# Corner products of a deformable convolution moved from VectorE to GpSimd, in place between its gathers, on one Trainium2 core

## The reference, cut to what matters

```python
# one sample: four corners, each with a weight
return gather(y0, x0) * (wy0 * wx0) + gather(y0, x0 + 1) * (wy0 * wx1) \
     + gather(y0 + 1, x0) * (wy1 * wx0) + gather(y0 + 1, x0 + 1) * (wy1 * wx1)
...
samp = _bilinear(h, y, x) * mask[:, None]
out = jnp.einsum('bckhw,ock->bohw', samp, w2.reshape(w2.shape[0], w2.shape[1], 9))
```

## Time and profile before

| what | value |
|---|---|
| median of the timed runs | 629.05 us (3 runs, 628.83 to 629.80) |
| span of the profiled execution, first to last instruction | 852.6 us |
| the profiled execution's own time around its span | not shown |
| busy: PE, DVE, ACT, POOL | 531.5, 353.6, 277.5, 283.4 us |
| POOL's gathers (L309), 288 | 282.2 us busy |
| DVE's products (L1167), 32 | 43.5 us busy |
| DVE's sums (L1180), 32 | 68.9 us busy |

### The profile page before, as it was taken

How to read it: one execution, slowest core, us unless ns; L and a number is a source line. 1 busy time by engine, 2 the same in 40 slices (tenths; PEclk the granted TensorE clock), 3 DMA queues, 4 the chain that set the end, 5 groups by cost and what they waited for, 6 DMA issues and landing times.

```text
span 852.6 us, 7735 instructions
## 1 busy us (share of the span) xinstructions
PE 531.5 (62%) x2840; PEld 362.9 (43%) x2840; DVE 353.6 (41%) x462; ACT 277.5 (33%) x402; POOL 283.4 (33%) x296
## 2 busy tenths in 40 slices
PE   5789930117883065026604897271859998999797
PEld 2445410113542033014502665151636785678576
DVE  4244420002671193129400586151347984752243
ACT  1436510005550041104100554130235633554353
POOL 0000477750037477734775006565520000000000
PEclk8697975558996578556756899585889999999899
DMA  4000111110001121100211001111100000000000
GB/s 166 0 1 1 52 52 53 52 40 26 1 22 53 37 63 52 52 26 22 76 52 43 1 2 40 43 41 43 59 22 0 0 25 0 1 1 16 10 1 25
DMA packets 15298, 27.11 MB, mean 32 GB/s; under 512 B 4900, under 2 KB 9256, under 8 KB 15144
## 3 DMA queue, kind: packets, MB, share of 16 engines
q0 software_dynamic: 9216, 18.89, 7.8%
q1 hardware_dynamic: 5768, 6.20, 2.2%
q10 hardware_dynamic: 288, 1.67, 0.5%
HBM read 22.41 MB, written 4.33 MB: 31 GB/s over the span
## 4 chain that ended last, share of the span: by engine, by line
PE 41%; another core or an unknown queue 30%; DVE 11%; issue 8%; ACT 7%; DVEq 2%; DMA 1%; ACTq 0%
PE ys L559 6%; PE yy L581 5%; PE xq L346 5%; DVE samples L1180 3%; PE yy L572 3%; DVE neg_max L1086 2%; ACT expT L805 2%; PE ys L479 2%; PE xq L319 2%; PE yy L319 2%; PE ys L319 2%; PE xs L325 2%; DVE weighed L1167 2%; PE xq L389 1%
## 5 line engine op out<-in xcount | busy, mean ns | idle before, releaser
L309 POOL DMA_INDIRECT got<-cell_table,rows_cur x288 | 282.2, 980 | 247.5 <-DVE weighed L1167 149.3
L346 PE MATMUL xq<-vT,expT 128*128 128x129 f32 x512 | 68.8, 294 | 14.9 <-ACT oT L898 7.3
L581 PE MATMUL yy<-v3T,probsT 128*128 128x128 f32 x512 | 65.1, 282 | 16.2 <-issue 15.3
L346 PEld LDWEIGHTS xq<-vT,expT 128*128 128x128 f32 x512 | 66.8, 210 | 19.5 <-issue 9.5
L581 PEld LDWEIGHTS yy<-v3T,probsT 128*128 128x128 f32 x512 | 61.7, 196 | 24.5 <-issue 20.2
L1180 DVE TENSOR_REDUCE samples<-weighed 128x288 f32<-128x1152 f32 x32 | 68.9, 2153 | 2.2 <-issue 0.7
L559 PE MATMUL ys<-k,q_offs 128*128 128x512 f32 x112 | 55.1, 616 | 1.3 <-ACT k L924 1.3
L1264 DVE TENSOR_REDUCE neg_max<-ys 128x1 f32<-128x1024 f32 x28 | 34.2, 1222 | 38.6 <-PE ys L559 35.7
L1210 DVE RECIPROCAL inv<-xq 128x1 f32<-128x1 f32 x32 | 5.3, 167 | 103.2 <-remote 68.6
L479 PE MATMUL ys<-samplesT,wts 96*128 96x512 f32 x48 | 29.8, 772 | 27.7 <-issue 27.1
L470 PE MATMUL yy<-wts,samples 128*96 128x128 f32 x72 | 14.1, 313 | 52.2 <-ACT samplesT L800 43.5
(11 more groups left out here) (186 smaller groups left out, 875.4 us busy)
## 6 DMA issues: line engine op xcount, KB each, us to landing
got<-cell_table,rows_cur POOLq DMA_INDIRECT x288
cell_table<-tabS SPq DMA_DIRECT2D x4, 512.0 KB
xall<-x_dram SPq DMA_DIRECT2D x3, 512.0 KB, 9.3
out_dram<-cells SPq DMA_DIRECT2D x3, 512.0 KB, 2.7
wts<-weights_dram ACTq DMA_DIRECT2D x1, 1120.5 KB, 8.9
xall<-x_dram ACTq DMA_DIRECT2D x1, 512.0 KB, 5.0
out_dram<-cells SPq DMA_DIRECT2D x2, 256.0 KB, 2.0
wts<-weights_dram SPq DMA_DIRECT2D x1, 289.0 KB, 4.8
```

The source lines that it names most:

```text
L309: nc.gpsimd.indirect_dma_start(got[:, t, k, :], None, table, bass.IndirectOffsetOnAxis(ap=rows_cur[:, n, at:at + 1], axis=0)).then_inc(got ...
L346: last = nc.tensor.matmul(to, expT[:, j, t * P:(t + 1) * P], vT[:, j, C - width:C + 1], start=j == 0, stop=j == TILES - 1)
L581: last = nc.tensor.matmul(yo[:, 0:C], probsT[:, j * P:(j + 1) * P], v3T[:, j, :], start=j == 0, stop=j == TILES - 1)
```

## The change

A POOL instruction multiplies the gathered corners in place, in the slot of `got`; DVE's product and its buffer go; DVE's sum waits for that product (`weighed`, now a semaphore), reads `got`, and releases slot and table after its drain. On POOL the product of tile t-1 stands behind the nine gathers of tile t; the last tile's product follows its own gathers. A wait for the corner weights stands once an element, ahead of the first product. In the second loop DVE's separate calls of `l1_weigh` go, and `l1_add` stays where it was; wherever `l1_samples` was called, `l1_add` is.

```diff
-        weighed = sb("weighed", [P, TAPS, CORNERS * R])
...
+        weighed = sem("weighed")
...
         @block.gpsimd
         def _(pool):
             rows_pair = rows_all[:, :, :].rearrange("p (a n) k -> p a n k", n=2)
+            weight_pair = corner_w[:, :, :, :].rearrange("p (a n) t k -> p a n t k", n=2)
+
+            def weigh(i, n, t):
+
+                pool.wait_ge(got_sem[t], 16 * TAPS * (2 * i + n + 1))
+                pool.sem_inc(pool_go, 1)
+                parts = got[:, t, :, :].rearrange("p k (c r) -> p (k c) r", r=R)
+                nc.gpsimd.tensor_tensor(parts, parts,
+                                        weight_pair[:, bass.ds(i, 1), n, t, :].rearrange("p a (k b) -> p (a k) b", b=1)
+                                        .to_broadcast([P, TAPS * CORNERS, R]), ALU.mult).then_inc(weighed, 1)
...
                             nc.gpsimd.indirect_dma_start(
                                 got[:, t, k, :], None, table,
                                 bass.IndirectOffsetOnAxis(ap=rows_cur[:, n, at:at + 1], axis=0)).then_inc(got_sem[t], 16)
+                        if t == 1:
+                            pool.wait_ge(corner_ready, 2 * i + n + 1)
+                            pool.sem_inc(pool_go, 1)
+                        if t:
+                            weigh(i, n, t - 1)
+                    weigh(i, n, TILES - 1)
...
-            def l1_weigh(i, t):
-
-                dve.wait_ge(got_sem[t], 16 * TAPS * (i + 1))
-                w = corner_w[:, bass.ds(i, 1), t, :].rearrange("p b k -> p (b k)")
-                nc.vector.tensor_tensor(weighed[:, :, :].rearrange("p k (c r) -> p (k c) r", r=R),
-                                        got[:, t, :, :].rearrange("p k (c r) -> p (k c) r", r=R),
-                                        w.rearrange("p (k a) -> p k a", a=1).to_broadcast([P, TAPS * CORNERS, R]),
-                                        ALU.mult).then_inc(slot_free, 1)
-                dve.drain()
+            def l1_add(i, t, early=False):
+
+                dve.wait_ge(weighed, TILES * i + t + 1)
+                if t >= 2 or early:
+
+                    dve.wait_ge(st_mm, TILES * i + t - 1)
+                nc.vector.tensor_reduce(samples[:, t % 2, :].rearrange("p (k r) -> p k r", r=R),
+                                        got[:, t, :, :].rearrange("p k (c r) -> p k r c", r=R),
+                                        axis=X, op=ALU.add).then_inc(sample_ready, 1)
+                dve.drain()
+                dve.sem_inc(slot_free, 1)
                 if t == TILES - 1:
                     dve.sem_inc(table_free, 1)
...
-                    if SAMPLES and t >= 3:
-                        l1_weigh(c, t - start)
...
-                                l1_samples(c, 6)
-                            if n == 3:
-                                l1_weigh(c, 7)
+                                l1_add(c, 6)
                             if n == 4:
                                 l1_add(c, 7)
...
              for t in range(4, TILES):
-                l1_samples(0, t)
+                l1_add(0, t)
             for t in range(2):
-                l1_samples(1, t, early=True)
+                l1_add(1, t, early=True)
             l1_conv2(0)
             l1_end(0)
             l1_coordinates(BATCH - 1, xp)
```

More of the change, by code:

```diff
@@ L1103, in l0_denominators @@
                 if samples_too:
-                    l1_samples(0, 0)
+                    l1_add(0, 0)
                 dve.wait_ge(d4_mm, i + 1)
@@ L1107, in l0_denominators @@
                 if samples_too:
-                    l1_samples(0, 1)
-                    l1_samples(0, 2)
+                    l1_add(0, 1)
+                    l1_add(0, 2)
                 dve.wait_ge(d_mm, i + 1)
@@ L1112, in l0_denominators @@
                 if samples_too:
-                    l1_samples(0, 3)
+                    l1_add(0, 3)
             def l0_end(i):
@@ L1160, in l1_coordinates @@
                 last.then_inc(corner_ready, 1)
-            def l1_weigh(i, t):
-                dve.wait_ge(got_sem[t], 16 * TAPS * (i + 1))
-                w = corner_w[:, bass.ds(i, 1), t, :].rearrange("p b k -> p (b k)")
-                nc.vector.tensor_tensor(weighed[:, :, :].rearrange("p k (c r) -> p (k c) r", r=R),
-                                        got[:, t, :, :].rearrange("p k (c r) -> p (k c) r", r=R),
-                                        w.rearrange("p (k a) -> p k a", a=1).to_broadcast([P, TAPS * CORNERS, R]),
-                                        ALU.mult).then_inc(slot_free, 1)
-                dve.drain()
-                if t == TILES - 1:
-                    dve.sem_inc(table_free, 1)
             def l1_add(i, t, early=False):
+                dve.wait_ge(weighed, TILES * i + t + 1)
                 if t >= 2 or early:
@@ L1180, in l1_add @@
                 nc.vector.tensor_reduce(samples[:, t % 2, :].rearrange("p (k r) -> p k r", r=R),
-                                        weighed[:, :, :].rearrange("p k (c r) -> p k r c", r=R),
+                                        got[:, t, :, :].rearrange("p k (c r) -> p k r c", r=R),
                                         axis=X, op=ALU.add).then_inc(sample_ready, 1)
                 dve.drain()
-            def l1_samples(i, t, early=False):
-                l1_weigh(i, t)
-                l1_add(i, t, early)
+                dve.sem_inc(slot_free, 1)
+                if t == TILES - 1:
+                    dve.sem_inc(table_free, 1)
             def l1_conv2(i):
@@ L1331, in second_loop_step @@
                 if SAMPLES:
-                    l1_samples(c, TILES - start)
+                    l1_add(c, TILES - start)
                 if L3 and L2:
```

## The result

The changed kernel takes 676.69 us (median of 4 runs, 675.23 to 677.85) against 628.94 us for the kernel before on the same chip: a ratio of 1.0784, 95% interval 1.0756 to 1.0813. The forecast was 712 us, with a range of 665 to 748, and "slower". The sign and the range hold; the size of the loss was forecast as 83 us and is 48.

The account below looks back on a forecast made before the run. Before: bound by the chain over PE, DVE and ACT, with POOL 19 us in hand. After: POOL's 94.2 + 467.2 = 561.4, plus 147.6 to the end, is 709.0; with 3 us allowed, 712 us, range 665 to 748.

Parts of the forecast that it names:

- The standstills: Stretches between 94.2 and 631 us where PE, DVE and ACT do nothing; claimed to exist only in the profiled execution.
- Rival (a): Gathers in timed runs start 0.94 us apart, not 1.25, so the kernel gets faster, 620 us; chance 5%.
- The allowance of 3 us around the span: Time that a timed run was assumed to have outside the profiled span: 3 us added to the sum.
- POOL's chain: Gathers, products and landing waits in a row on POOL: 115.9 us per element, 467.2 us for four with turns.
- first and last term: Time before the first gather, 94.2 us, and from DVE's last sum to the end, 147.6 us.
- The place of the wait: DVE was to stand most of 40 us waiting for POOL's products, from element 0's tile 7 to element 1's tile 1.
- The product: Each of 32 multiplications on POOL, between gathers: 2.6 us, the middle of 1.36 and 3.9, plus 0.3 us start.
- The landing: Wait before each element's last product until its own tile's gathered data has arrived: 2.0 us an element.
- the main case: Product from 1.9 to 3.3 us and the profile's gather pace: 690 to 734 us; chance 60%.
- rival (b): Late, but less: product near DVE's 1.36 us (672 us) or gather pace between 0.97 and 1.25 us; chance 18%.
- POOL has 19 us in hand over the whole kernel: Before the change, POOL can be done at 460.6 us and must be done by 479.9 us.
- DVE's relief: Removing 32 products and drains, 43.5 us busy, from DVE; at most 17 us of it on the path.

Follow-up runs that it names:

- late sums: Kernel after, with the two early sums of element 1 moved behind the second convolution's split, the residual sum and element 3's coordinates: 676.26 us, ratio 1.0726.
- undisturbed execution: Kernel before run again with no edit, for a profile without standstills: 627.18 us, ratio 0.9995, profiled span 624.9 us.
- the pieces: Kernel before with DVE's product cut into two, four or nine instructions: 618.53, 616.87 and 620.82 us, ratios 0.9825, 0.9815 and 0.9867.

## Why the prediction was right, and where it was not

- **The standstills** were read rightly: they were in one profiled execution only, and POOL's pace of 1.25 us is the same without them. Rival (a), a faster pace in timed runs, is out: in the kernel after the profiled execution took 675.87 us, among the timed ones, with gathers at 1.25 us. The allowance of 3 us around the span was near: the time of that execution is 1.8 us above its span.
- **POOL's chain sets the time**: shown by the doubled product (+64 us for 68.5), the halved one (-27 for 31) and the late sums (no clear change). The forecast's first and last term, 94.2 and 147.6, came out as 94.2 and 148.6.
- **The place of the wait** was right as well: DVE stands 34 us before the first two sums of element 1, forecast as most of 40. That this wait of itself costs time was not shown: moving the work out from behind it gained nothing that shows clearly, 4 us at most by the ratios.
- **The terms mis-sized** are those of the middle: forecast 561.4 for the end of the last product, measured 525.1. (1) The product: forecast 2.6 + 0.3 = 2.9 us per tile. Measured: tiles follow each other at 13.29 us, nine gathers are 11.24, so a product costs 2.05. The instruction is 2.14 us, and the further start that I had added doesn't exist: the 0.30 us between two gathers make way for some 0.02 and 0.16 around the product. That is 32 x 0.85 = 27.2 us of the 36.3 us. The value was a middle between two ends far apart, and the truth lay nearer to DVE's row. (2) The landing: forecast 2.0 us an element, measured nothing, 8 us. I had priced the wait by itself and not seen that the product of tile 6 stands ahead of it in the queue and covers it; where nothing covers it, it costs 1.7 us. (3) The rest, 1.1 us, is in gathers a little less delayed than those of the first element and in shorter turns.
- **How much of it was luck:** the conditions of the main case held, a product from 1.9 to 3.3 us and a pace of 1.25, and still 677 us lies below its 690 to 734. The range holds because it was drawn down to 665 for rival (b), a product near 1.36 us or a pace below 1.25, and neither of these came. A product of 2.14 us alone takes the sum from 712 to 697; the rest of the way are a start and a landing that the sum had and the kernel has not: 32 x (2.14 + 0.30 - 2.05) = 12.5 us, and 8 us.
- **The step that failed outright** is "POOL has 19 us in hand over the whole kernel". It has none. It was made from an undisturbed pace, 90.7 us an element, of which I had noted that it held a single delayed gather and that 10 to 11 us of delay were in the trace; I then left this delay out of the time of before and credited 4 us of it at most to the change. In the undisturbed execution the 19.3 us went as follows: 13.6 into gathers longer than those of the first element, less 1.1 because the first gather starts earlier; 1.6 into the landing of the last tile, which stands between the last gather and DVE's product; and 5.1 because the deadline itself was too late, set by the timed 629.05 us where the span is 624.9, and by 149.2 us behind the product where it is 150.1. The step also took a wait in a profile with standstills for a sign ("POOL waits for slots, the others seldom for it"); undisturbed, POOL waits for no slot after its first gather, and DVE's products wait 40 us for the gathers. The error hardly touched the forecast, because the sum was made from POOL's chain alone and not as before plus a difference; but it made the reading of before wrong, and it hid what the pieces gain.
- **Where the 48 us come from**, as 49.2 between the spans 674.1 and 624.9: products on POOL 32 x 2.05 = +65.6; gathers freed of DVE's products 288 x (958 - 1007) ns = -14.1; the rest, -2.3, lies at both ends of POOL's stretch (+1.0 and -2.7) and in the turns.
- **DVE's relief** (at most 17 us on the path, by the chain with standstills) was worth nothing of its own: 43 us of the same work with one input gave the same ratio as none (0.9705 and 0.9712).

## What to carry to other kernels

Before work is moved to an engine, find the stretch in which that engine runs without a pause, and compare its end with the deadline at the delayed pace, not at the clean one; a share of 47% of the span can be a full load. An operation on VectorE with two inputs in SBUF costs GpSimd's gathers too: cut it in two, or give it one input, before it is moved. And price a wait in its place in the queue: what stands ahead of it may cover it, as nine gathers did here for 28 landings and the product of the tile before for the other four, 53 us in all.

## What was not expected of the hardware

- A gather that meets a DVE product with two SBUF inputs waits for about the rest of it (0.94 to 1.78 us in the rows shown) unless both start together; a DVE reduction of the same length from the same buffer doesn't delay it (mean 952 ns). The Trainium skill's rule in "SBUF — State Buffer", section "Who interferes with whom", that two-input operations contend with GpSimd instructions that read SBUF and reductions never do, agrees with both, if a gather, which takes its row numbers from SBUF, counts as such a reader. The same section infers that a two-input operation leaves the making of descriptors alone; for these gathers it does not hold.
- It goes the other way too: four short DVE instructions of the kernel after last until POOL's product has ended (a CAST 1.95 us instead of 0.2).
- A GpSimd product of two f32 operands, one of them broadcast, costs 0.19 us + 1.69 ns an element (from 576 and 1152 elements), 1.57 times DVE's (2138 against 1363 ns). The Trainium skill's "GPSIMD Engine Reference", section 3.1, gives 1.96 times for an addition and, scaled from its 4497 ns for 2048 elements, an estimate of 2.5 us; here it is less.
- Cutting that DVE product in two removes 35 of the 55 ns that it adds to a mean gather (1007 ns against 952 with a reduction in its place), in four no more (973), and in nine less (984 ns).
